# Weight preparation for three stages in one block, kept copies moved behind other work, and the residual of the feed-forward placed ahead of the next x's scales

## The reference

```
def fp4_quant_dequant(x):                  # blocks of 16 along the last dimension
    scale = max(max(abs(xb)) / 6, 1e-12)
    q = GRID[searchsorted(MID, abs(xb / scale))] * sign(xb) * scale
h = silu(fp4(x) @ fp4(w_gate).T) * (fp4(x) @ fp4(w_up).T)      # 256 -> 704
y = fp4(h) @ fp4(w_down).T                                      # 704 -> 256
```

## Time and profile before

| | |
|---|---|
| median of three runs | 3728.39 us (3726.32 to 3740.59) |
| profiled execution | 3728.92 us, of which the span is 3727.1 us |
| PE busy | 3135.2 us, 84% |
| DVE busy | 2741.7 us, 74% |
| ACT busy | 2198.9 us, 59% |
| POOL busy | 1114.8 us, 30% |
| mean granted clock of TensorE | 0.922 of full speed |

### The profile page before, as it was taken

One profiled execution on the slowest core, in us unless ns is written; L12 is line 12 of the kernel. 1 busy time (PEld: TensorE's weight loads), 2 busy tenths in 40 slices (PEclk: granted clock), 3 DMA queues, 4 the chain that ended last, 5 costly groups with the idle time before them and its releaser, 6 DMA issues. The chain is left out here.

```text
span 3727.1 us, 70608 instructions
## 1 busy us (share of the span) xinstructions
PE 3135.2 (84%) x24024; PEld 2426.1 (65%) x24024; DVE 2741.7 (74%) x7223; ACT 2198.9 (59%) x5352; POOL 1114.8 (30%) x658
## 2 busy tenths in 40 slices
PE   6899898998991899997488888888888886499998
PEld 4666666666661799886265655556655554488888
DVE  4676676766765898992378878877887885599996
ACT  4666676676671344441377777777777775244443
POOL 1000000000000555551233433334343333355554
PEclk9999999999995999998699999999999997799999
DMA  5244343442421000001343434444343442211100
GB/s 88 43 67 60 48 72 50 62 65 43 61 37 63 6 18 18 18 18 67 48 55 55 72 58 69 63 71 67 58 69 63 64 62 40 74 35 35 35 29 23
DMA packets 134182, 190.46 MB, mean 51 GB/s; under 512 B 15126, under 2 KB 81558, under 8 KB 133142
## 3 DMA queue, kind: packets, MB, share of 16 engines
q1 hardware_dynamic: 133830, 185.95, 29.6%
HBM read 45.65 MB, written 28.84 MB: 20 GB/s over the span
## 5 line engine op out<-in xcount | busy, mean ns | idle before, releaser
L408 ACT ACTIVATE a_probs<-a_probs,a_negmax 128x176 f32<-128x176 f32 (+4 forms) x1024 | 501.6, 490 | 333.7 <-DVE a_negmax L331 333.3
L331 DVE CUSTOM_DVE_ANT_0 a_probs<-a_mask,a_score 128x176 f32<-128x176 f32 (+4 forms) x1024 | 403.8, 400 | 224.7 <-PE a_score L482 96.4
L493 PE MATMUL a_turned<-ident,a_probs 128*128 128x128 f32 (+1 forms) x2176 | 430.0, 290 | 77.8 <-DVE a_pT L340 70.9
L1765 ACT ACTIVATE b_u<-b_u,b_negmax 128x512 f32<-128x512 f32 x512 | 366.3, 716 | 98.2 <-DVE b_negmax L1645 97.7
L1645 DVE CUSTOM_DVE_ANT_0 b_u<-b_u,b_score 128x512 f32<-128x512 f32 x512 | 340.0, 681 | 101.5 <-PE b_score L1891 100.5
L1091 PE MATMUL f_y_bank<-f_wdT,f_hqT 128*128 128x256 f32 x1536 | 358.7, 383 | 44.6 <-DVE xs L964 42.5
L1900 PE MATMUL b_turned<-ident,b_u 128*128 128x128 f32 x2048 | 334.7, 290 | 72.8 <-DVE b_pT L1651 44.2
L1637 DVE SCALAR_TENSOR_TENSOR b_u<-b_u,b_score 128x1024 f32<-128x1024 f32 x256 | 309.1, 1214 | 90.8 <-ACT b_u L1758 88.9
L1758 ACT ACTIVATE b_u<-b_score 128x1024 f32<-128x1024 f32 x256 | 262.2, 1024 | 156.9 <-PE b_score L1881 156.6
L1900 PEld LDWEIGHTS b_turned<-ident,b_u 128*128 128x128 f32 x2048 | 250.4, 148 | 159.1 <-issue 124.1
L1091 PEld LDWEIGHTS f_y_bank<-f_wdT,f_hqT 128*128 128x128 f32 x1536 | 284.6, 190 | 92.6 <-DVE xs L964 55.0
(11 more groups left out here) (233 smaller groups left out, 7022.6 us busy)
## 6 DMA issues: line engine op xcount, KB each, us to landing
b_stack<-b_part SPq DMA_DIRECT2D x192, 256.0 KB, 8.3
a_stack_q<-a_part SPq DMA_DIRECT2D x192, 128.0 KB, 4.3
a_stack_k<-a_part SPq DMA_DIRECT2D x192, 128.0 KB, 5.8
xs<-in_x_dram SPq DMA_DIRECT2D x16, 512.0 KB, 8.4
x_before_b<-xs SPq DMA_DIRECT2D x16, 512.0 KB, 2.9
b_xin<-x_before_b SPq DMA_DIRECT2D x16, 512.0 KB, 12.3
b_xres<-x_before_b SPq DMA_DIRECT2D x16, 512.0 KB, 3.9
x_after_b<-b_xres SPq DMA_DIRECT2D x16, 512.0 KB, 2.9
```

The lines of the kernel that those rows point to most:

```text
L331: dve.tensor_tensor_reduce(out=probs[:, n % 2, j, 0:keys(n)], in0=mask_of(n), in1=score[j][:, 0:keys(n)], scale=-1.0, scalar=3.0e38, op0=A ...
L408: act.activation(probs[:, n % 2, j, 0:keys(n)], probs[:, n % 2, j, 0:keys(n)], ACT.Exp, bias=negmax[:, n, j:j + 1], scale=-1.0, accum_out= ...
L493: m = nc.tensor.transpose(turned[j % 2][0:rows, u, :], chunk(n, probs[:, n % 2, j, :], u), ident[:])
L1765: act.activation(u[:, n, j, :], u[:, n, j, :], ACT.Exp, bias=negmax[:, n, j:j + 1], scale=-1.0, accum_out=sums[:, c, t, j:j + 1]).then_inc ...
```

## The change

1. `prepare_ffn` and `prepare_b` become one block, `prepare`, between attention a and the first feed-forward. The weights that attention b uses lie in SBUF from the start (`b_weights`), those of attention a share their tiles.
2. In it the dividing and the scaling of the matrices are done by POOL, the high part of gate and up is moved by ScalarE, `u` and `mag` have two buffers, and the folding of attention b's weights stands between the turns on TensorE.
3. `copy` is gone. The kept weights are stored by SyncE at the start of the first feed-forward and fetched in attention b, ahead of the last store, into the room of the first half of `u`.
4. In `ffn`, in slots 0 and 1 the residual stands ahead of `front_scales` and `front_round`.

The diff, cut to its core (the operations of the quantisation are the same as before):

```diff
-def prepare_ffn(nc, ident, wguT, wdT, w_gate, w_up, w_down):
+def prepare(nc, ident, wguT, wdT, a, w):
...
         @block.sync
         def _(sp):
+            for (n, p, f, src), dst, s in zip(items, raw, s_raw):
                 sp.dma_start(dst[:], src).then_inc(s, 16)
+            for dst, name in loads:
+                sp.dma_start(dst[:], a[name]).then_inc(s_w, 16)
...
         @block.gpsimd
+            pool.memset(wdT[:, IC - 1, :], 0.0).then_inc(s_deq, 1)
+            divide(0)
+            divide(1)
+            scale(0)
+            pool.wait_ge(s_deq, 2)
+            divide(2)
+            scale(1)
+            scale(2)
...
         @block.vector
+            scales(0)
+            scales(1)
+            mark(0)
+            scales(2)
+            mark(1)
+            for n in range(4):
+                move(n)
+            mark(2)
+            dve.wait_ge(s_deq, 1)
+            for n in range(4, len(turns)):
+                move(n)
+            dve.wait_ge(s_w, 16 * len(loads))
+            dve.tensor_scalar(out=w["wq"][:], in0=wq_in[:], scalar1=CW_SCALE, scalar2=None, op0=ALU.mult)
+            dve.tensor_scalar(out=w["bq"][:], in0=bq_in[:], scalar1=CW_SCALE, scalar2=None, op0=ALU.mult)
+            dve.wait_ge(s_mm, 1)
...
         @block.scalar
+            for i in range(3):
+                magnitude(i)
+            for n in range(8):
+                high(n)
...
         @block.tensor
+            pe.wait_ge(s_w, 16 * len(loads))
+            fold_heads()
+            fold_up()
+            for n in range(4):
+                turn(n)
+            fold_down()
+            for n in range(4, len(turns)):
+                turn(n)
...
-def ffn(nc, tag, xs, ident, consts, wguT, wdT, x_from, x_to):
+def ffn(nc, tag, xs, ident, consts, wguT, wdT, x_from, x_to, kept):
...
             ahead = 4
+            for dst, src in kept:
+                sp.dma_start(dst, src).then_inc(s_out, 16)
...
-            sp.wait_ge(s_out, 16 * SEQS)
+            sp.wait_ge(s_out, 16 * (SEQS + len(kept)))
...
                     if behind(1):
                         round_hidden(*behind(1))
+                    if behind(3):
+                        residual(*behind(3))
                     if n == 0 and has(s + 1):
                         front_scales(s + 1)
                     if n == 1 and has(s + 1):
                         front_round(s + 1)
-                    if behind(3):
-                        residual(*behind(3))
...
             b_bodies(sp, body, 2)
+            sp.wait_ge(s_turn, 32 * (SEQS - 1) + 16)
+            sp.sem_inc(s_steps, 1)
+            for dst, src in kept:
+                sp.dma_start(dst, src).then_inc(s_kept, 16)
             store_x(SEQS - 1)
+            sp.wait_ge(s_kept, 16 * len(kept))
             sp.wait_ge(s_store, 16 * SEQS)
...
-            prepare_ffn(nc, ident, wguT, wdT, a["w_gate"], a["w_up"], a["w_down"])
-            copy(nc, "keep", [(kept_gu, wguT[:].bitcast(FP32)), (kept_d, wdT[:])])
-            ffn(nc, "f1", xs, ident, consts, wguT, wdT, None, x_before_b)
-        attention_b(nc, ident, consts, a, x_before_b, x_after_b)
+            prepare(nc, ident, wguT, wdT, a, w)
+            ffn(nc, "f1", xs, ident, consts, wguT, wdT, None, x_before_b,
+                [(kept_gu, wguT[:].bitcast(FP32)), (kept_d, wdT[:])])
```

More of the change, by code:

```diff
@@ new lines, in prepare @@
+        w1T = sb("w1T", [P, FC, H])
+        wm = sb("wm", [P, FC, NQ])
+        b1 = sb("b1", [P, FC])
+        bm = sb("bm", [P, NQ])
+        wqoT = sb("wqoT", [P, FC, NQ])
+        bqo = sb("bqo", [P, FC])
+        w2 = sb("w2", [P, FC, H])
+        wq_in = sb("wq_in", [P, KC, H])
+        bq_in = sb("bq_in", [P, KC])
+        bank = [pb(f"bank{i}", [P, SEQ]) for i in range(2)]
+        fold = pb("fold", [P, KC, P])
+        bias = pb("bias", [P, 16])
+        up = pb("up", [P, KC, NQ])
+        down = pb("down", [P, H])
@@ new lines, in scale @@
+            def scale(i):
+                r, f, nb = shape(i)
+                pool.wait_ge(s_mark, 2 * i + 2)
+                pool.tensor_tensor(out=blocks(raw[i][:]), in0=blocks(u[r, i % 2, 0:f]),
+                                   in1=spread(nscale[r, i, 0:nb], nb), op=ALU.mult).then_inc(s_deq, 1)
+            pool.memset(wdT[:, IC - 1, :], 0.0).then_inc(s_deq, 1)
[4 more added lines that the diff above has]
+            divide(2)
@@ L642, in _, with scales @@
-            dve.wait_ge(s_pad, 1)
-            for n, (w, k, half) in enumerate(turns):
+            def scales(i):
+                r, f, nb = shape(i)
+                dve.wait_ge(s_raw[i], 16)
+                dve.tensor_reduce(out=amax[r, i, 0:nb], in_=blocks(raw[i][:]), axis=AX.X, op=ALU.max,
+                                  apply_absolute_value=True).then_inc(s_v, 1)
+                dve.wait_ge(s_v, 3 * i + 1)
+                dve.tensor_scalar(out=nscale[r, i, 0:nb], in0=amax[r, i, 0:nb], scalar1=-SIXTH, scalar2=-SCALE_MIN,
+                                  op0=ALU.mult, op1=ALU.min).then_inc(s_v, 1)
+                dve.wait_ge(s_v, 3 * i + 2)
+                dve.tensor_scalar(out=inv[r, i, 0:nb], in0=nscale[r, i, 0:nb], scalar1=-TIE_DOWN, scalar2=None,
+                                  op0=ALU.mult).then_inc(s_v, 1)
+                dve.wait_ge(s_v, 3 * i + 3)
+                dve.reciprocal(out=inv[r, i, 0:nb], in_=inv[r, i, 0:nb]).then_inc(s_inv, 1)
@@ new lines, in _ @@
+            for n in range(4, len(turns)):
[4 more added lines that the diff above has]
+            dve.wait_ge(s_mm, 1)
+            dve.tensor_copy(w["wqk"][:], fold[:])
+            dve.tensor_tensor(out=w["bqk"][:], in0=bias[:, 0:1], in1=bc[:], op=ALU.add)
@@ L656, in _, with magnitude @@
+            dve.tensor_copy(w["wm"][:], up[:])
+            dve.tensor_tensor(out=w["bm"][:], in0=bias[:, 8:8 + NQ], in1=bm[:], op=ALU.add)
+            dve.tensor_copy(w["wff"][:], down[0:NQ, :])
+            dve.tensor_tensor(out=w["rows"][:, 4, :], in0=row1[:], in1=w["rows"][:, 4, :], op=ALU.add)
+            dve.tensor_tensor(out=w["rows"][:, 5, :], in0=row2[:], in1=w["rows"][:, 5, :], op=ALU.add).then_inc(s_mv, 1)
+            dve.wait_ge(s_mv, 1)
         @block.scalar
         def _(act):
-            for i, (n, p, f, _) in enumerate(items):
+            def magnitude(i):
+                r, f, nb = shape(i)
```

294 lines of the change are left out of this document (121 added, 173 removed).

## The result

The changed kernel takes 3714.46 us (median of seven runs, 3707.94 to 3716.36); the kernel before, on the same chip, 3728.39 (seven runs, 3723.77 to 3740.59). The ratio is 0.9958, 95% interval 0.9945 to 0.9972: 14 us faster. The forecast was 3688, its range ended at 3706, so it was too low by 26 us and the time lies outside the range.

The account below looks back on a forecast made before the run. Bounds: exposed stretches at three joints; in the feed-forward a closed chain through VectorE, POOL's xq and TensorE, with VectorE and POOL taking turns. 3728.9 - 12.05 - 43.8 - 6.5 + 21.3 = 3687.9, forecast 3688; range 3650 to 3706 (own 3680 to 3700).

Parts of the forecast that it names:

- The fetch hidden: Before the second feed-forward: the fetch of kept weights, issued ahead of the last store, leaves the span; -12.05 us.
- Rival C: Second feed-forward's weight fetch not hidden, SyncE reaching it late or the last store landing behind it; +12, 3700 us; chance 0.06.
- The separate block: Before the second attention: the weight block goes, so the first x is fetched where the first load stood; -43.8 us.
- The joint block: Between attention a and the first feed-forward: copy wait gone, folding added inside; -6.5 us taken, bounds -12 to +3.
- The turns in slot 0 and slot 1: Feed-forward loops: the earlier residual changes VectorE's and POOL's turns, delaying xq by 0.92 and 0.33 us; +21.3 us in all.
- Rival D: Feed-forward loops: TensorE's one stand of about 2.4 us per period lowers its clock, making the kernel slower than before; chance 0.03.
- Rival A: Feed-forward loops: TensorE was the bound and the earlier residual frees its 55 us of waits; 3611.5 us; chance 0.07.
- B: Feed-forward loops: neither tie lost, only slot 1's changed turns remain, periods of 30.95 us; 3662 us; chance 0.14.
- the ties: Feed-forward slot 0: VectorE's small operation and POOL's operation issued almost together; losing costs 1.13 us, in 12 of 28 periods before.

Follow-up runs that it names:

- e3: The changed kernel with the residual moved ahead only in slot 0 (of the scales), in slot 1 behind the rounding as before; 3684.6 us.
- e4: The changed kernel with the residual moved ahead only in slot 1 (of the rounding of x), in slot 0 behind the scales; 3672.2 us.
- e1: The changed kernel with the residual back behind the scales and the rounding, so only the change of the blocks; 3662.2 us.
- e2: The kernel before with the residual ahead of the scales and the rounding, nothing else; 3776.0 us.
- e5: The changed kernel with four unused 128x256 products on TensorE behind the down product of slot 2, filling its stand; 3682.7 us.
- e10: e1 with x_nscale on POOL, xq ahead of POOL's hidden divide, and the residual ahead of both scales and rounding; 3669.3 us.

## Why the prediction was wrong

Point by point, by its own steps:

- The fetch hidden: right, -12.0 (forecast -12.05). Rival C did not happen.
- The separate block: right, -43.8.
- The joint block: right, -7.8 (-6.5), and in its inner times too. Counted from the first largest-value operation (L682), the sketch had the second fold begin at 33.3 us, the ten last turns over at 53.8 and the statistics at 57.0; they came at 34.6, 54.0 and 56.5.
- The turns in slot 0 and slot 1: right. Periods of 31.87 forecast, 31.93 measured where the clock stays; +0.87 and +0.41 by e3 and e4, forecast +0.92 and +0.33. Over the 26 periods this is 26 x 31.93 - 808.6 = +21.6; the forecast for 28 was +21.3. e1 and e2 show that the residual, and nothing else of the change, makes it.
- **The step that failed**: in the sum the loop runs with the granted clock of the kernel before, 1.00, and the longer stand costs nothing but itself. In the trace 17 of 26 periods have a fall behind the stand, at 1.54 us: +26.2. The last period of each feed-forward, behind the 26, has one too (+1.6 each, 55.85 us from its xq to the last residual instead of 54.25). Together +29.4, and that is the miss: 3688 + 29.4 = 3717, measured 3714.5. e5 shows the cause: the same order and the same turns with the stand filled have none of it (granted clock 1.00 in the window of the earlier trace rows, where the changed kernel has 0.96).
- Rival D had the clock, and the place: behind the one stand of 2.4 us. It was given the wrong form: low in every one of the 28 periods or in none, with 0.03. How long the clock stays low behind such a stand, and what that costs, no trace of the kernel before shows; in the changed kernel it is 0.50 for about 3.4 us, and such a fall costs 1.54 us and comes in two periods of three. "TensorE would still be busy for more than nine tenths" was my ground against it, and that ground was no evidence: it is busy for 0.93 of the time in the changed kernel, with falls, and for 0.93 in e4, without.
- What I took from the trace for the clock was a stretch with stands of 0.84 in a good period and of 1.09 and 0.72 in one with a lost turn ("two of about 1" fits only the second kind). It says that these are free. It says nothing of one of 2.4, and what a trace does not show has to be bounded from both sides. With D as a bound on the forecast's own case instead of a far rival, the range would have held the time.
- Rival A (TensorE the bound, 3611.5) and B (ties not lost, 3662) did not happen: in the window of the earlier trace rows each of 14 periods loses exactly one turn in slot 0.

The rows at 1471.38 are one more of the ties: L1042 and POOL's L987 are issued within 0.01 us of each other, and VectorE's gets through in 0.20. L1042 does so in 7 of the 28 periods of the changed kernel, and then L1044 waits (1.38 or 1.39, otherwise 0.18); in the other 21 L1042 itself waits (1.43 or 1.44).

Two things stay open: why two periods in three fall and not all, at stands of 2.02 and 2.41 alike, and what else than the length of the stand decides, at 1.8 (7 of 26 in e3, none of 17 in e10) and at 2.15 (8 of 28 at the ends of the feed-forwards). The runs give the counts, not a cause.

## What to carry to other kernels

Moving an operation so that an engine waits "once instead of twice" is not neutral for TensorE: one long stand can cost more than two short ones with the same sum (here 1.54 us behind 2.41 in one piece, nothing behind 1.35 and 1.09), since the clock can fall behind it; look for the longest single stand, not for the busy share. Moving work ahead on a busy engine pays only if what waits for it comes last: the same move of the residual cost 0.41 us per period while xq came last, and gave 0.18 once it did not (in the profiled periods; the medians show neither gain nor loss there). And a mechanism that the trace can neither show nor exclude belongs into the range as a part of the likeliest case, not beside it as a rival that comes in full or not at all.

## What the runs showed of the hardware that I had not expected

- The granted clock falls from 1.00 to 0.50 behind a single stand of 2.02 us in a loop in which TensorE is otherwise busy, 17 times of 26, and never in 26 behind one of 1.60. A stand of 2.41 in the same place changes neither how often it falls nor the price, 1.54 us. In another place a stand of 2.15 had a fall behind it in 8 of 28 cases.
- Useless products can pay: 1.9 us of them per period made the kernel 25 to 32 us faster (by the ratios, by the medians), and 0.5 us of them did nothing.
- The same stage, attention a, ran at a mean clock of 0.94 in one execution and 0.96 in another, which is 10 us of span, and over fourteen executions it ended between 1117 and 1132 us: a difference of less than that between two single executions says nothing.
- When operations of VectorE and POOL are issued within 0.02 us of each other, which goes first is worth 1.13 us, and it does not come out the same way each time (12 lost of 28 in the kernel before, 16 in e1, where the order in the loop is the same).
